# Two engines share a row mask: half of each channel's scaling on ScalarE, half on VectorE

## The reference, cut to what matters

```python
m = src_mask.astype(jnp.float32)
mask = (m[:, :, None] * m[:, None, :])[..., None]
left = (xn @ W_left + b_left) * mask
right = (xn @ W_right + b_right) * mask
left = left * jax.nn.sigmoid(xn @ W_lgate + b_lgate)
right = right * jax.nn.sigmoid(xn @ W_rgate + b_rgate)
...
out = jnp.einsum('bkid,bkjd->bijd', left, right)
out = _layernorm(out, out_norm_scale, out_norm_bias) * out_gate
```

## Time and profile before

| what | value |
|---|---|
| median of three runs | 1854.53 us (1853.44 to 1859.64) |
| profiled execution | 1866.85 us, of which the span is 1865.1 us |
| mixing of the fourth stage, first mask scaling to last sum | 1540.7 to 1710.1 us of the span |
| busy share of the span | PE 77%, DVE 68%, ACT 51%, POOL 19% |
| granted clock of TensorE, mean of the profiled execution | 0.913 of full speed |

### The profile page before, as it was taken

One profiled execution on the slowest core, in us unless ns is written; L12 is line 12 of the kernel. 1 busy time (PEld: TensorE's weight loads), 2 busy tenths in 40 slices (PEclk: granted clock), 3 DMA queues, 4 the chain that ended last, 5 costly groups with the idle time before them and its releaser, 6 DMA issues. The chain is left out here.

```text
span 1865.1 us, 30335 instructions
## 1 busy us (share of the span) xinstructions
PE 1427.8 (77%) x8768; PEld 738.0 (40%) x8768; DVE 1270.3 (68%) x2030; ACT 943.4 (51%) x1542; POOL 345.5 (19%) x288
## 2 busy tenths in 40 slices
PE   5597499757687476869988997565969977774797
PEld 4444333212275222223337996122223325553343
DVE  3874479228777599138975777799049976767664
ACT  3785444644333243657875665000848863443355
POOL 0000078110000088000000000465000000000465
PEclk9998799889988699889998999899979989998899
DMA  5657511006677442019998996775038879996998
GB/s 206 234 119 197 162 50 31 1 20 176 181 248 239 111 95 47 1 53 352 335 347 281 304 302 200 281 276 180 4 115 342 343 292 300 301 290 197 350 411 330
DMA packets 234894, 387.16 MB, mean 208 GB/s; under 512 B 21667, under 2 KB 162854, under 8 KB 229414
## 3 DMA queue, kind: packets, MB, share of 16 engines
q1 hardware_dynamic: 177558, 320.56, 51.9%
q10 hardware_dynamic: 57232, 65.29, 10.1%
HBM read 194.26 MB, written 190.32 MB: 206 GB/s over the span
## 5 line engine op out<-in xcount | busy, mean ns | idle before, releaser
L1034 PE MATMUL bank<-work 128*128 128x256 f32 x1408 | 348.0, 397 | 63.4 <-ACT work L1066 43.3
L1386 POOL TENSOR_TENSOR xT<-xT,work 128x512 f32 (+1 forms) x192 | 241.7, 1269 | 817.4 <-DVE work L1440 817.3
L730 ACT ACTIVATE work<-bank,bias 128x512 f32<-128x512 f32 x448 | 286.4, 685 | 142.4 <-PE bank L627 68.6
L1034 PEld LDWEIGHTS bank<-work 128*128 128x128 f32 x1408 | 267.5, 198 | 116.8 <-ACT work L1066 24.4
L804 DVE SCALAR_TENSOR_TENSOR work<-bank,bias,work 128x512 f32<-128x512 f32 x320 | 236.6, 748 | 36.1 <-PE bank L627 29.0
L627 PE MATMUL bank<-work,w 64*64 64x512 f32 x2048 | 257.9, 607 | 1.5 <-DVE work L804 1.5
L1059 ACT COPY work<-bank 128x512 f32<-128x512 f32 x176 | 103.0, 585 | 235.4 <-PE bank L1034 134.5
L721 ACT ACTIVATE work<-bank,fold 128x512 f32<-128x512 f32 x192 | 116.5, 688 | 191.5 <-PE bank L620 191.3
L794 DVE SCALAR_TENSOR_TENSOR work<-xT,fold,bank 128x512 f32<-128x512 f32 x192 | 141.3, 739 | 101.4 <-PE bank L660 101.4
L1123 DVE TENSOR_TENSOR work<-work 128x512 f32<-128x512 f32 x176 | 121.3, 689 | 74.5 <-ACT work L1059 73.8
L1594 POOL TENSOR_TENSOR xT<-xT,work 128x512 f32<-128x512 f32 x64 | 80.1, 1272 | 407.3 <-ACT work L1565 407.3
(11 more groups left out here) (137 smaller groups left out, 1925.6 us busy)
## 6 DMA issues: line engine op xcount, KB each, us to landing
work<-hidden_rows SPq DMA_DIRECT2D x352, 256.0 KB, 3.7
hidden_rows<-work SPq DMA_DIRECT2D x128, 512.0 KB, 3.7
z_rows<-work ACTq DMA_DIRECT2D x176, 256.0 KB, 3.5
work<-z_rows SPq DMA_DIRECT2D x48, 512.0 KB, 7.4
work<-in_x SPq DMA_DIRECT2D x64, 256.0 KB, 4.0
hidden_rows<-work SPq DMA_DIRECT2D x128, 128.0 KB, 2.3
work<-z_rows SPq DMA_DIRECT2D x16, 1024.0 KB
work<-gate_rows SPq DMA_DIRECT2D x16, 1024.0 KB, 4.9
```

The source lines that it names most:

```text
L730: nc.scalar.activation(result(t, column), GB[n % len(GB)][:, :], ACT.Sigmoid, bias=bias(name)).then_inc(gate_sb, 1)
L1034: mm = pe.matmul(ZB[b % 2][:, r * N:r * N + N], a[:, kk, r * P:r * P + P], x[:, kk, :], start=(kk == 0), stop=(kk == 1))
L1386: pool.tensor_tensor(x, x, term[:, ring(j, q, TERMS), :], ALU.add).then_inc(x_sb, 1)
```

## The change

DVE scales only the first half of the right operand (columns 0 to 255). The second half is scaled by a new ACT instruction, an Identity activation with `msq` as scale. ACT does it in its own step for channel c, for channel c+2, ahead of the copy, the square and the store of channel c-1; the first two channels are scaled before the loop. PE waits for both halves on two semaphores in place of one.

```diff
@@ PE, ready
                 elif row_mask and o:
-                    pe.wait_ge(masked_b, 2 * c + 2)
+                    pe.wait_ge(scaled0, c + 1)
+                    pe.wait_ge(scaled1, c + 1)
@@ ACT
+            def scaled(c, b):
+
+                if row_mask:
+                    act.wait_ge(landed[b], (c - b) * 8 + 32)
+                    x = loaded(1, b)[:, N:2 * N]
+                    nc.scalar.activation(x, x, ACT.Identity, scale=msq[:, 1:2]).then_inc(scaled1, 1)
+
@@
             def channel(c, b):
+                if exists(c + 2):
+                    scaled(c + 2, (b + 2) % 4)
                 turned(c, b)
                 if exists(c - 1):
                     finished(c - 1, (b - 1) % 4)
 
+            for b in range(2):
+                scaled(b, b)
             each_channel(act.Fori, channel)
             finished(channels - 1, 3)
@@ DVE, masked
                 if row_mask:
 
                     dve.wait_ge(landed[b], (c - b) * 8 + 32)
-                    for kk in range(2):
-                        x = loaded(1, b)[:, kk * N:kk * N + N]
-                        dve.tensor_scalar(x, x, msq[:, kk:kk + 1], None, ALU.mult).then_inc(masked_b, 1)
+                    x = loaded(1, b)[:, 0:N]
+                    dve.tensor_scalar(x, x, msq[:, 0:1], None, ALU.mult).then_inc(scaled0, 1)
```

More of the change, by code:

```diff
@@ L955, in mix @@
     with ExitStack() as ctx:
-        (masked_a, masked_b, turn_mm, ta_sb, tb_sb, z_mm, z_sb, sq_sb, s1_sb, s2_sb, begun, shifted) = core.sems(
-            f"mix{layer}{part}", "masked_a masked_b turn_mm ta_sb tb_sb z_mm z_sb sq_sb s1_sb s2_sb begun shifted")
+        (masked_a, masked_b, scaled0, scaled1, turn_mm, ta_sb, tb_sb, z_mm, z_sb, sq_sb, s1_sb, s2_sb, begun,
+         shifted) = core.sems(f"mix{layer}{part}", "masked_a masked_b scaled0 scaled1 turn_mm ta_sb tb_sb z_mm z_sb "
+                              "sq_sb s1_sb s2_sb begun shifted")
         landed = core.sems(f"mix{layer}{part}", "in0 in1 in2 in3")
```

## The result

The changed kernel takes 1870.87 us (median of 6 runs, 1867.76 to 1876.62) against 1856.80 us of the kernel before (6 runs, 1853.44 to 1861.47). The ratio is 1.0076, 95% interval 1.0055 to 1.0098: 14 us slower, 10 to 18. The forecast was 1857, no change, with a range from 1847 to 1868.

A forecast was written before the change was run, and what follows sets the result against it. A two-channel loop through the stores was taken to bind the fourth stage; a new three-channel loop adds 1.8 us and the start 0.5, so 1854.53 + 2.3 = 1856.8, rounded 1857, range 1847 to 1868.

The forecast's parts named there:

- The stores' loop over two channels: Fourth stage before: copy, its store, the landing, copy of c+2; 5.28 us over two channels, 2.64 a channel, binds.
- the DMA engines are nearly full: Fourth stage before: DMA share 0.94 at 301 GB/s, so 320 GB/s when full and landing time mostly queueing.
- the faster rival: Fourth stage: spreading helps the DMA engines, loads land in 3.0 us, 2.48 us a channel, 1846.6 us; chance 0.14.
- the new wait: ACT waits for load c+2 before copying c-1, which pushes back the second copy of each pair by 1.8 us.
- the end of the pairs: Fourth stage: channels that ran in pairs will be spread out, one landing, one copy, at even distance.
- the loop over three channels: Landing of load c+2, scaling, copy, square, product, issue of load c+5, landing: 7.94 us, 2.65 a channel.
- three of its four terms: Scaling on ACT 0.41 us, copy start to product start 1.32, product start to issue of the load 2.14.
- With even spacing I take 3.5: 4.07 us: Issue of both loads to landing: 0.57 us plus the third stage's median 3.5, where the fourth had 3.9.
- rival 1: Fourth stage: loads keep 3.9 us, 8.34 us over three channels, 2.78 a channel, +10 us, 1864.6; chance 0.30.
- The start: Start of the fourth stage: out(0) stands behind load 3, the reduction giving the shift starts 0.5 us later, once.
- DVE's relief: DVE loses 64 instructions of 350 ns, 22.4 us of work; costed at nothing, hidden by the waiting for DMA.

The follow-up runs named there:

- run 6: Kernel before with four buffers in place of two for the copies of the product in the fourth stage; 1829.99 us, ratio 0.9830 to the kernel before.
- run 8: Changed kernel, ACT's scaling behind copy, square and store: with eight load and four copy buffers 1823.38 us (0.9819 to kernel before); with four and four 1837.45 us (0.9898).
- Run 1: Changed kernel with ACT's scaling of channel c+2 moved behind the copy, square and store of channel c-1; ratio 0.9998 to the kernel before.
- run 2: Kernel before plus only ACT's wait for the load of channel c+2 ahead of the copy of c-1; ratio 1.0057 to the kernel before.
- run 5: Eight load buffers in place of four in the fourth stage: changed kernel 1.0003, kernel before 1.0007, both as ratios to the unedited kernel before.
- run 4: Kernel before plus one unused Identity activation a channel on ACT at the scaling's place, without the wait; ratio 1.0005 to the kernel before.
- run 9: Kernel before with eight unused transposes of x a channel added on PE in the fourth stage; ratio 1.0014 to the kernel before.
- Run 10: Kernel before with the eight added transposes, loads held until the transposes behind the product of c-4; ratio 1.0005 to the kernel before.

## Why the prediction was wrong, point by point

- **Right: what bound the kernel before.** The stores' loop over two channels; run 6 opened it and the time fell by 30 us.
- **Wrong beside it: "the DMA engines are nearly full".** I divided 301 GB/s by the share 0.94 and took 320 GB/s for full. Runs 6 and 8 moved 380 and 383 GB/s. It misled me twice more: I took landing times for queueing that would shrink to the third stage's when the pace evened out, and I set the faster rival's floor at 2.46 us where 2.04 was to be had with more buffers.
- **Right: the new wait, the end of the pairs, the loop over three channels, and three of its four terms.** Runs 1, 2 and 5 show the loop: it goes when it is closed over four or seven channels, and stays with the wait alone. The instruction costs 508 ns where 511 was taken. That also agrees with the estimate from the Trainium skill's page "ScalarE: Activation LUTs" (493 ns). The page's rule against multiplications on ScalarE gave the right sign, but the work alone is not what costs: runs 1 and 4 have it on ACT and lose nothing.
- **The step that failed: "With even spacing I take 3.5: 4.07 us".** The landing of a pair is 4.48 us in the changed kernel. The mechanism was right and this term mis-sized: 0.41/3 = 0.14 us a channel, 8 us in 60. Two things were wrong in it. First, the reading: 3.5 and 3.9 are medians over first and second loads together, and it is the second that counts. In the third stage the two hardly differ, so 4.07 fits it (4.09). In the changed kernel the same recipe on its own median gives 0.57 + 3.6 = 4.17, and 4.48 is measured. Second, the premise: the third stage's latency was taken to come with even spacing. The copies came 2.07 to 3.99 us apart, and run 9 shows that evenly issued loads can still take 4.91. Run 10 shows that the order of issue matters: in the third stage the store goes out 0.13 to 0.27 us ahead of the pair, and with that order the fourth stage has the same 4.08.
- **How much of the 0.41 us the order explains is open.** In the changed kernel the store goes out behind the first load in 31 of the 56 pairs, which land after 4.60 us on average, and ahead of it or with it in 25, which land after 4.34. So order goes with 0.26 us there, and even with the store ahead a pair takes 0.25 us longer than in the third stage. The uneven spacing is left as a suspect; no run separates it.
- **The account.** With 4.48 the forecast's own sum is (0.41 + 1.32 + 2.14 + 4.48)/3 = 2.78 us a channel, +0.16 x 60 + 0.5 = +10 us. Measured are 2.80 and 14 us (10 to 18). These are also the numbers of rival 1, which had a chance of 0.30 and 1864.6 us, but that is luck. Rival 1 is the loop at today's latency, and it took 4.47 us for it by the same mixed median; a pair really took 4.90 in the kernel before. With that its sum is 8.77, 2.92 us a channel and some +18.5 us. The latency did get shorter, as the forecast said, by half of the way from 4.90 to the third stage's 4.09. The range ended at 1868, below rival 1's own upper end of 1869. The start was within its 0.5 us: from the first scaling to the reduction that gives the shift it is 6.7 us, against 6.5 before.
- **Right: DVE's relief is worth nothing.** Run 1 halves DVE's mask work and equals the kernel before, and run 4, where DVE keeps it all and ACT has the same work more, equals it too.
- **Open:** run 2 cost 10.6 us where the loop without the scaling term gives 2.65 us a channel (1.30 + 2.14 + 4.51), some 2 us; the trace has 2.72. The stores' loop of 2.62 lies close beneath it, and I put the rest down to the two loops disturbing each other. No run shows that.

## What to carry to other kernels

When a wait is put into an engine's list, count the channels round the loop that it closes and divide the loop's latency by that number: here moving the wait by three instructions turned a division by three into one by four, and 14 us into none. In a stage where all engines idle, look for such loops and count buffers; two more copy buffers were worth twice what the change lost, and the DMA share was no evidence that there was nothing to gain. A latency borrowed from another stage comes with that stage's order and spacing of issue, so compare both before borrowing, and where a loop waits for the last of several transfers, read the landing of the last one and not the median of all.

## What the runs showed of the hardware

- A DMA share of 0.94 to 0.97 was reached at 301 GB/s; the same pattern of 256 KB loads and stores moved 380 to 383 GB/s at a share of 1.09 once more transfers were allowed in flight.
- At a pace of 2.6 us a channel, two loads of 256 KB issued 0.57 us apart landed 4.08 us after the first issue with a 256 KB store issued 0.12 to 0.27 us ahead of them, and 4.91 us after it in the run with the store mostly 0.6 to 1.6 us behind. The stores themselves took a median of 3.2 against 4.5 us. The second run began with landings of 3.9 to 4.2 us at the same order, so the order alone does not set the time; why it matters is not shown.
